# An attention and expert kernel: the first rows are normalised before the scaled weights, the other batches are turned before the first score step, and GpSimd multiplies the decay of twelve heads for ScalarE's logarithms

## The reference

```python
xn = _layernorm(x)                                   # x: 8 x 512 x 128
q, k, v = split(xn @ w_attn)                         # 16 heads of 8 channels
decay = softplus(decay_raw)                          # one number for each head
log1p_dist = log1p(maximum(i - j, 0))
logw = -log1p(decay[:, None, None] * log1p_dist)     # one 512 x 512 mask for each head
scores = q @ k.T / sqrt(8) + causal + logw
att = softmax(scores) @ v @ w_proj
out = x + att + two experts of eight (SiLU between two weight matrices), weighted by the router
```

## Time and profile before

| what | value |
|---|---|
| median of 3 runs | 505.39 us (504.28 to 505.66) |
| the profiled execution | 506.12 us, its span 504.4 us |
| busy share of the span | PE 95%, DVE 73%, POOL 73%, ACT 67% |
| chain that ended last, by engine | PE 69%, DVE 17%, ACT 10%, waiting for nothing shown 2% |
| prologue and first slots | first score step on DVE at 23.4 us, first exponential at 36.4 us |
| expert slots | about 328 to 466 us |

### The profile page before, as it was taken

One profiled execution on the slowest core, in us unless ns is written; L12 is line 12 of the kernel. 1 busy time (PEld: TensorE's weight loads), 2 busy tenths in 40 slices (PEclk: granted clock), 3 DMA queues, 4 the chain that ended last, 5 costly groups with the idle time before them and its releaser, 6 DMA issues.

```text
span 504.4 us, 13425 instructions
## 1 busy us (share of the span) xinstructions
PE 478.1 (95%) x4294; PEld 346.7 (69%) x4294; DVE 365.7 (73%) x1407; ACT 336.6 (67%) x621; POOL 366.2 (73%) x591
## 2 busy tenths in 40 slices
PE   6769899999999999999999999989999999999997
PEld 5645465555664665566566556689999999999564
DVE  7888989988999989989889897733333333333887
ACT  4789878888888888887988888752233233232762
POOL 3587987889888889889889888734454554555784
PEclk9998999999999999999999999999999999999999
DMA  6479790780470461353255153877676777672634
GB/s 188 126 278 286 201 215 16 213 199 18 133 215 28 143 182 57 122 158 102 90 159 138 51 183 112 227 223 238 199 210 208 210 208 207 191 216 69 246 118 140
DMA packets 72755, 82.24 MB, mean 163 GB/s; under 512 B 8638, under 2 KB 52704, under 8 KB 72688
## 3 DMA queue, kind: packets, MB, share of 16 engines
q1 hardware_dynamic: 68368, 72.91, 50.3%
q0 software_dynamic: 4320, 8.47, 4.7%
HBM read 49.94 MB, written 31.86 MB: 162 GB/s over the span
## 4 chain that ended last, share of the span: by engine, by line
PE 69%; DVE 17%; ACT 10%; issue 2%; DMA 1%; SPq 0%; ACTq 0%; DVEq 0%
PE psT L1498 22%; PE psT L1585 13%; PE ps L1558 12%; PE psO L1518 11%; DVE scores L1268 8%; PE ps L1470 6%; ACT probs L1008 4%; ACT scores L965 3%; PE psM L1446 2%; DVE x_all L608 2%; PE ps L1549 1%; ACT values L992 1%; DVE xt L1122 1%; DMA w_qkv<-w_attn 1%; DVE probs L1054 1%
## 5 line engine op out<-in xcount | busy, mean ns | idle before, releaser
L1268 DVE CUSTOM_DVE_ANT_0 scores<-ps,wdist 128x256 f32<-128x256 f32 (+3 forms) x512 | 217.3, 485 | 22.6 <-PE ps L1470 21.8
L1008 ACT ACTIVATE probs<-psT 128x512 f32<-128x512 f32 x320 | 173.8, 597 | 50.3 <-PE psT L1498 49.1
L875 POOL TENSOR_SCALAR scores<-scores,row_max 128x256 f32<-128x256 f32 (+3 forms) x388 | 185.3, 493 | 29.2 <-DVE row_max L1268 28.1
L1498 PE MATMUL psT<-ident,scores 128*128 128x128 f32 x1280 | 176.3, 281 | 5.7 <-ACT probs L1008 5.6
L1498 PEld LDWEIGHTS psT<-ident,scores 128*128 128x128 f32 x1280 | 137.7, 141 | 64.0 <-issue 46.3
L894 POOL DMA_INDIRECT picked_dram<-scores,row_ring x71 | 69.8, 983 | 70.0 <-DVE scores L1349 66.8
L1017 ACT ACTIVATE scores<-ps 128x512 f32<-128x512 f32 x71 | 42.3, 598 | 91.4 <-PE ps L1558 91.4
L1518 PE MATMUL psO<-probs,values 128*32 128x512 f32 (+3 forms) x1024 | 88.4, 441 | 0.0
L965 ACT ACTIVATE scores<-scores,row_max 128x512 f32<-128x512 f32 x124 | 83.0, 727 | 0.0
L1585 PE MATMUL psT<-xn_all,scores 128*128 x568 | 75.4, 276 | 1.6 <-ACT scores L1017 1.6
L1558 PE MATMUL ps<-scores,wdist 128*128 128x128 f32 x568 | 74.9, 275 | 0.6 <-DMA wdist<-w1t 0.6
(11 more groups left out here) (169 smaller groups left out, 295.3 us busy)
## 6 DMA issues: line engine op xcount, KB each, us to landing
wdist<-w1t SPq DMA_DIRECT2D x71, 256.0 KB, 3.4
k_rows<-k_dram SPq DMA_DIRECT2D x64, 96.0 KB, 3.0
q_rows<-q_dram SPq DMA_DIRECT2D x64, 96.0 KB, 2.9
row_ring<-rows_dram SPq DMA_DIRECT2D x71, 65.0 KB, 2.9
rows_dram<-row_ring SPq DMA_DIRECT2D x6, 650.0 KB, 6.3
k_dram<-k_parts SPq DMA_DIRECT2D x7, 384.0 KB, 2.4
q_dram<-q_parts SPq DMA_DIRECT2D x7, 384.0 KB, 2.6
xn_all<-picked_dram SPq DMA_DIRECT2D x4, 512.0 KB, 7.4
```

The source lines that it names most:

```text
L875: last = nc.gpsimd.tensor_scalar(part, part, -1.0, row_max[:, r, tile, quad:quad + 1], ALU.mult, ALU.add)
L1008: nc.scalar.activation(probs[:, at.ring(2), w, :], psT[:, w % 2], ACT.Exp, scale=-1.0).then_inc(exp_ready, 1)
L1268: last = nc.vector.tensor_tensor_reduce(out=scores[:, r, u, col:col + n], in0=bank[:, col:col + n], in1=wdist[:, at.g * QUADS + quad, SEQ ...
L1498: last = nc.tensor.transpose(psT[:, w % 2, place * P:(place + 1) * P], scores[:, at.ring(2), u, col + key * P:col + (key + 1) * P], ident[:])
```

## The change

- The scaled weights become a step of their own (WQ) and stand behind NX in the list, so DVE normalises the first batch's rows ahead of them. PE has two matmuls of WU behind WC instead of eight. SP issues `w_attn` ahead of the decays.
- The list ahead of slot 0 is written anew: the statistics of batches 1 to 3 are taken in two portions around the split of keys and queries, the turns (XB) of all batches and the values (VL) of batch 4 stand ahead of the first score step, and the last statistics (four tiles), their seven small instructions and their power move into slot 1. The second RT, its RO and the seven LC move to the end of slot 1.
- Heads 4 to 15: a new step LM on POOL multiplies `log_dist` with the decay (twelve instructions, each 128 x 512), and ACT takes the logarithm of two heads in one instruction. Heads 0 to 3 stay as they were.
- In slot 29, MI stands ahead of ACT's last two subtractions (SA) instead of behind them. In slot 32, PE's second PV step stands behind the second pair of turns.

```diff
-EARLY = {0: {1: (("XB", 24), ("VL", 16), ("LN", 7)),
+EARLY = {0: {1: (("VL", 20), ("LN", 8)),
...
+         1: {0: (("BN", 0, 3, 28, 32),), 1: (("RS", 3),), 3: (("CZ", 2),),
+             4: (("RT", 1), ("RO", 1)) + tuple(("LC", b * GROUPS) for b in range(1, BATCH)) + (("CZ", 3),)}}
...
     step("PV", n - 2, NGROUP, 0)
-    step("PV", n - 2, NGROUP, 1)
+    if n != NGROUP:
+        step("PV", n - 2, NGROUP, 1)
...
     p1(2)
     p1(3)
+    if n == NGROUP:
+        step("PV", n - 2, NGROUP, 1)
...
     step("TE", n - 1, NGROUP, 8, 10)
+    if n == EXPERT_SLOT - 1:
+        steps.append(("MI", 0))
     if n >= GROUPS_BY_POOL:
         step("SA", n, NGROUP, (6, 7))
...
 PROLOGUE = [
-    ("BN", 0, 0, 0, 4), ("RS", 0), ("WU", 5), ("WC", 0), ("WU", 8), ("NX", 0), ("LN", 0), ("LN", 1), ("XB", 0), ("LN", 2),
+    ("BN", 0, 0, 0, 4), ("RS", 0), ("LM", 4), ("LM", 6), ("LM", 8), ("LM", 10), ("LM", 12), ("LM", 14), ("WU", 5), ("WC", 0), ("WU", 2), ("NX", 0), ("WQ", 0), ("LN", 0), ("LN", 1), ("XB", 0),
...
                 sp.dma_start(x_all[:, 0:TILES, :], x_rows(0)).then_inc(first_x_loaded, 16)
+                sp.dma_start(w_qkv[:], w_attn).then_inc(w_loaded, 16)
                 sp.dma_start(decay_in[:], decay_raw.rearrange("(a h) -> a h", a=1).broadcast_to([P, HEADS])
                              ).then_inc(decay_loaded, 16)
-                sp.dma_start(w_qkv[:], w_attn).then_inc(w_loaded, 16)
...
+                def decay_step(at):
+
+                    pool.wait_ge(act_init, 3)
+                    pool.wait_ge(decay_ready, 1)
+                    pool.wait_ge(xn_ready, 1)
+                    for h in range(at.c, at.c + 2):
+                        last = nc.gpsimd.tensor_scalar(wdist[:, h, :], log_dist, decay[:, h:h + 1], None, ALU.mult)
+                    last.then_inc(wdist_scaled, 1)
...
-                    nc.scalar.activation(wdist[:, h, :], log_dist, ACT.Ln, bias=1.0, scale=decay[:, h:h + 1]
-                                         ).then_inc(wdist_ready, 1)
+                    if h < QUADS:
+                        nc.scalar.activation(wdist[:, h, :], log_dist, ACT.Ln, bias=1.0, scale=decay[:, h:h + 1]
+                                             ).then_inc(wdist_ready, 1)
+                        return
+                    act.wait_ge(wdist_scaled, h // 2 - 1)
+                    nc.scalar.activation(wdist[:, h:h + 2, :], wdist[:, h:h + 2, :], ACT.Ln, bias=1.0).then_inc(wdist_ready, 2)
...
-                        scaled_weights()
                         dve.wait_ge(dve_init, 1)
...
-                def scaled_weights():
+                def scaled_weights(at):
...
-                    pe.wait_ge(vo_free, BATCH if n else 2)
+                    pe.wait_ge(vo_free, BATCH if n else 4)
...
-                    if b == 3:
+                    if b == 4:
                         pe.wait_ge(rstd_copied, 1)
-                    if b == 4:
                         pe.wait_ge(misc_free, MISC["KA", 0] + 1)
```

More of the change, by code:

```diff
@@ L85 @@
 TOPK = 2
-EARLY = {0: {1: (("XB", 24), ("VL", 16), ("LN", 7)),
-             2: (("XB", 28), ("VL", 20), ("LN", 8), ("LN", 9), ("CZ", 1)),
-             3: (("VL", 24), ("LN", 10), ("LN", 11)),
-             4: (("VL", 28), ("RT", 1)) + tuple(("LN", h) for h in range(12, 16)) + (("TL", 0), ("XN", 4), ("RO", 1)) + tuple(
+EARLY = {0: {1: (("VL", 20), ("LN", 8)),
+             2: (("VL", 24), ("LN", 10), ("CZ", 1)),
+             3: (("VL", 28),) + (("LN", 12), ("LN", 14)) + (("TL", 0),),
+             4: (("XN", 4),) + tuple(
                  (kind, b * GROUPS) for kind, b in (("VS", 4), ("VS", 5), ("VS", 6), ("VS", 7), ("XS", 2), ("XS", 3), ("XS", 4),
                                                     ("XS", 5), ("XS", 6), ("XS", 7)))},
-         1: {2: tuple(("LC", b * GROUPS) for b in range(1, BATCH)) + (("CZ", 2),), 4: (("CZ", 3),)}}
+         1: {0: (("BN", 0, 3, 28, 32),), 1: (("RS", 3),), 3: (("CZ", 2),),
+             4: (("RT", 1), ("RO", 1)) + tuple(("LC", b * GROUPS) for b in range(1, BATCH)) + (("CZ", 3),)}}
 FIRST_ROWS_SLOT, ROW_TILES = 1, 4
@@ L246, in slot_steps @@
     steps.extend(("PA", 0, *part) for part in SUMS.get(n, ()))
-    if n == EXPERT_SLOT - 1:
-        steps.append(("MI", 0))
     if (n - 2) % PAIR == PAIR - 1:
@@ L476, in build @@
         wdist_ready = sem("wdist_ready")
+        wdist_scaled = sem("wdist_scaled")
         wdist_causal = sem("wdist_causal")
@@ L860, in causal_step @@
                                             ).then_inc(wdist_causal, 1)
-                run_prologue({"RS": rstd_step, "CZ": causal_step})
+                run_prologue({"RS": rstd_step, "CZ": causal_step, "LM": decay_step})
                 def less_step(at, i):
@@ L900, in _ @@
                 last_row = nc.gpsimd.to_reg(BATCH * SEQ * TOPK - 1)
-                run_slots({"RS": rstd_step, "CZ": causal_step, "LC": logits_step, "P1": less_step, "NR": rows_step, "SC": send_step,
+                run_slots({"RS": rstd_step, "CZ": causal_step, "LM": decay_step, "LC": logits_step, "P1": less_step, "NR": rows_step, "SC": send_step,
                            "MD": slot_send, "PA": add_picked(nc.gpsimd, pool, POOL_BATCHES, pool_summed)})
@@ L1005, in exp_step @@
                         if at.c == 1 and w == UNITS - 1:
-                            act.wait_ge(wdist_ready, HEADS)
+                            act.wait_ge(wdist_scaled, HEADS // 2 - 2)
                         act.wait_ge(turned, at.groups(UNITS, w + 1))
@@ L1127, in _ @@
                 number_parts["BN"] = norm_stats
-                run_prologue({**number_parts, "BN": norm_stats, "NX": normalise})
+                run_prologue({**number_parts, "BN": norm_stats, "WQ": scaled_weights, "NX": normalise})
                 done = [0]
@@ L1439, in step @@
                             pe.wait_ge(xt_copied, 1)
+                            pe.wait_ge(centred_copied, 1)
                         if kind == "KA" and at.c > 0:
```

## The result

The changed kernel takes 518.24 us (median of 4 runs, 517.37 to 518.75), the kernel before beside it 505.52 us (4 runs): ratio 1.0251, 95% interval 1.0224 to 1.0277. It is slower by 2.5%, where 504.8 us was forecast. The profiled execution took 518.75 us with a span of 517.0 us, 12.6 more than before.

The account below looks back on a forecast made before the run. DVE was taken to set the pace up to 56.08 us, mostly PE after. Steps up to R1 netted 0.6 us, late edits 0: 506.12 - 0.6 = 505.5 profiled, 504.8 median; range 502.6 to 506.9.

Parts of the forecast that it names:

- step 3: POOL before the first scores: twelve multiplications at 0.70 us, power ending at 20.7, first scores at 23.4 against 23.44.
- Rival D: POOL's multiplications dearer, 1.16 us each, with DVE sharing its port; first scores at 28.9, total 510.3 us; chance 0.08.
- Step 1: Start of DVE: decays issued behind w_attn land at 5.6 us, bounds 4.60 to 6.11; normalised rows ready at 9.3.
- Step 2: PE's prologue: with fewer warm-ups batch 0's turns start at 9.4, 1.2 us sooner, and QL ends at 15.6.
- Rival C: PE's prologue: fewer warm-ups leave turns, keys and queries at 1.2 GHz; first scores at 25.2, total 506.5 us; chance 0.13.
- Steps 4 and 5: DVE in slot 0 and at slot 1's start: batch 1's scaling ends at 32.4, slot 1 starts 1.2 us sooner.
- Step 6: Work moved into slot 1: R1 waits for POOL's seven logits and comes at 45.5 us against 46.12.
- The late edits: MI before the expert slots and PV in slot 32: gain 0, at most 1.2 and 0.2 us.

Follow-up runs that it names:

- e1: Kernel before, with nine unread instructions added on POOL behind its first power to price each instruction form; 509.03 us in its one execution.
- e2: Changed kernel with the twelve POOL multiplications written as times decay, plus 0.0; median 509.90 us, ratio 1.0085 to the kernel before.
- e8: Changed kernel with plus 0.0 in the multiplications, decays issued first again and eight WU instead of two; 506.28 us, ratio 1.0007 to the kernel before.
- e6: Kernel before with only SP's order changed, w_attn issued ahead of the decays; 505.12 us, ratio 0.9975.
- e4: Kernel before with only MI moved ahead of ACT's last two subtractions; 505.25 us, ratio 0.9995.
- e3: Changed kernel without the POOL multiplications, ACT taking logarithms head by head with the decay as scale; 509.75 us, ratio 1.0074 to the kernel before.
- e9: Kernel before with w_attn issued ahead of the decays and two WU behind WC instead of eight; 510.50 us, ratio 1.0108.
- e14: Kernel before with two WU behind WC instead of eight, nothing else; 509.29 us, ratio 1.0082.
- e15: Changed kernel with six WU put behind the queries of batch 0, restoring PE's list length; 518.40 us, ratio 1.0247 to the kernel before.
- e13: Changed kernel with plus 0.0 in the multiplications and eight WU behind WC instead of two; 506.96 us, ratio 1.0024 to the kernel before.
- e10: Changed kernel without POOL multiplications, decays issued first, six WU put behind batch 0's queries; 505.26 us, ratio 1.0001 to the kernel before.

## Why the prediction was wrong

**The step that failed is step 3**, twelve multiplications on POOL at 0.70 us each, with an upper bound of 1.16. They took 1.54. To the 23.4 that was forecast for the first scores this adds 12 x 0.84 = 10.1; they began 0.7 sooner than thought (8.70 against 9.4), and the turns and values behind the power took about 2 longer, at the lower clock after PE's long wait: 23.4 + 10.1 - 0.7 + 2.0 = 34.8, as measured. The error was in calling the subtraction "a subtraction of the same form and size". The kernel writes it as times -1, plus the row's maximum: two operations; the multiplication has one. The row of the trace prints the same for both, so the instruction in the code had to be read too. The bound of 1.16 took only a price at 128 columns and left the price of a column as it was, while it is the price of a column that differs.

The Trainium skill, "GPSIMD Engine Reference", section 3.1, says that a loop body of up to two operations is limited by the ports, at 1.03 cycles per element; by that rule one operation would not be dearer than two. e1 shows 2.5 ns a column for one and the earlier trace rows 0.75 for two: the measurement decides.

Rival D named the right place and the right sign; its upper price of 1.16 was too low, and its reason, a shared port, is not what the rows show: e1's prices go by form, and the twelve in the changed kernel last 1.567 to 1.582 us each (they start 1.54 apart), beside a busy DVE and beside an idle one (DVE had no work from 22.9 to 33.3).

With the price right the forecast would still have been too low: e2, with 0.67 each, has a median of 509.90, above the forecast's range. What is left is the late decays with the lower clock (steps 1 and 2) and the shorter list for PE, for which the prediction has no term: e8, which puts the form, the warm-ups and the order of the loads right, is level with the kernel before. The other steps:

- **Step 1, decays** taken at 5.6, bounds 4.6 to 6.1: the profiled execution had 4.93, others with this order 4.75 to 6.43. The upper bound was too low. In the kernel before, where the rows wait for the scaled weights anyway, a landing at 5.79 did no harm (e6).
- **Step 2, turns sooner**: 8.54 for 9.4, QL at 14.80 for 15.6; right in this execution, but only where the clock is high. The 10.60 that the step starts from belongs to an execution in which `w_attn` landed late; e4, with the same prologue, has 9.29. Rival C, given 0.13, is what happened in the profiles of e3, e9, e14 and e15. Its price on the kernel before is part of e14's 0.8% and of e9's loss against e6, the part up to R1: 2.5 us in e9. The Trainium skill, "TensorE: Matmul & The Clock Gate", Part 1, has the throttled state as the default that activity releases. The runs agree: with six matmuls fewer the keys took 2.07 (e14), with them 1.12 (e13).
- **Steps 4 and 5**: slot 0 shorter by 0.4 and no wait for PE at the start of slot 1: from the first scores to slot 1 it was 8.8 (34.80 to 43.61) for a predicted 9.0, against 10.2 before.
- **Step 6**: R1 does wait for POOL's logits (idle 1.25), and comes 21.8 behind the first scores, predicted 22.1, before 22.7.
- **The late edits at nothing**: right for MI (e4). The PV edit was not tried alone; in the profile PE's last PV matmuls end at 510.06, ahead of DVE's sums at 510.43, as they did before (497.44 and 497.75).
- Not foreseen: that a shorter list for PE moves a load of instructions, and that 2.1 us are lost behind R1 with it.

## What to carry to other kernels

A price from the trace holds only for an instruction with the same operations, not only the same engine, shape and operands: read the line in the code as well as the row, and bound a price by the column if no row has the size. When a step is put ahead of others on an in-order engine, ask what it delays if it costs double; here one further operand (plus 0.0) would have cut the harm from 2.5% to 0.85% (e2). Warm-up matmuls that fill a wait look like idle work, but without six of them two kernels were 4 to 5 us slower (e14, e9); in e9's profile about half of that is lost up to R1, with PE's lower clock, and half far behind it, with the shorter list. Take one away only together with the wait it bridges, and look at the whole span. Before a row of the prologue is used as a base, look at a second execution: here the same prologue differed by 1.15 us.

## What was not expected of the hardware

- POOL's `tensor_scalar` with one operation takes 1.48 to 1.59 us for 128x512 float32 numbers, with two operations 0.69 to 0.80 (e1).
- Six matmuls fewer ahead of the first slot move a load of 16 KB of instructions, 300 us later, from 1.9 ahead of the last scatter to 0.3 to 1.1 behind it. SP, which waits for the scattered rows, goes on 0.5 to 1.0 later, and the rest of the program ends 1.9 later in the mean (eight kernels against ten; e10 and e15 move the packet back). That the packet holds up the rows on a DMA engine is the likely way, and was not shown.
- A broadcast load of 64 bytes to each partition, issued behind `w_attn`, was there for DVE at 4.75 to 6.43 us in different executions.
